# One half of the attention outputs divided on ScalarE instead of VectorE

## The chip, the core and the metric

The kernel runs on one core of a Trainium2 chip. The core has five engines with instruction streams of their own: TensorE (PE, matrix products, results into PSUM), VectorE (DVE), ScalarE (ACT), GpSimd (POOL) and SyncE (SP, which here only issues transfers). They wait for each other through semaphores. The metric is the device time of the whole program in microseconds (us), median of the runs shown.

## What is computed

Two sequences of 1024 tokens with 256 channels pass an attention layer, a residual with layer norm, a ternary linear layer and a second residual with layer norm:

```python
q = rmsnorm(rope(h @ Wq_c @ Wq_up), q_norm_w)       # 16 heads of 128
k_sw = rmsnorm(rope(h @ Wk), k_norm_w); v_sw = h @ Wv # one key/value head
ck = rmsnorm(h.reshape(b, nb, 16*256) @ W_comp)       # one key = value per 16 tokens
c_out  = attend(q @ ck^T * scale, blocks that end before the token, sink, ck)
sw_out = attend(50 * tanh(q @ k_sw^T * scale / 50), last 64 tokens, sink, v_sw)
attn = (c_out + sw_out in 4 groups @ Wg) @ Wo
x = layernorm(h + attn)
out = layernorm(x + x @ ternary(weight)^T + bias)
```

`attend` is a softmax with one more column, the head's sink, that takes part in the sum but has no value. Of importance here is `sw_out`, the window attention: the sum of exponentials times values, divided by the sum of the exponentials plus the sink's.

## The kernel before

**Tiles and stages.** After a preparation of some 75 us (keys, values, folded weights) the kernel goes through 16 tiles of 128 tokens. The function `step(i, front, mid, proj, ffn)` is written once for each engine and runs for i from -1 to 17. In one step, four tiles are under work: `front` makes the queries of tile i+1, `mid` does the attention of tile i, `proj` projects the attention output of tile i-1 and takes the first layer norm, `ffn` does the linear layer and second norm of tile i-2. The order on each engine is the order in which `step` issues its instructions; nothing reorders them. In this document "tile n" also names the step that has tile n in `mid`.

**Window attention of a tile.** The 128 tokens are two halves of 64 queries, c = 0 and 1. Each half sees 128 keys. With 16 heads a half has 1024 rows of scores; two heads of 64 queries fill 128 partitions, so a half is eight pairs. PE makes the scores (L582), ACT takes tanh and exp (L810, L814) into `E`, POOL multiplies by the mask (`mask(c)`, L1213) into `Pm`, and PE multiplies each pair by the values (`values(c)`, L665). A pair's result is 128 x 129 in PSUM: 128 output columns and, as the last one, the sum of the exponentials. The eight pairs lie in banks 4, 6 and 5, three, three and two in a bank, and both halves use the same three banks.

**Division (`divide(c)` on DVE).** DVE waits for the products (`p_pv`), adds the sink's term `e1` to the sums (`dn`, L1088), in half 0 also takes the reciprocals `rc` of the block attention's sums (L1092), takes the reciprocals `r8` (L1094), and multiplies the pairs by them with two instructions, 768 and 256 columns (`quotients`, L1102), into the float tile `ao`. `ao` and `Pm` lie in one room, which the trace names `room_wg`; `r8` is `r` in the trace and `room_wo` holds `PcT`, `y` and `x1`. `d_ao` tells that the half is done. Half 0 is rounded to 16 bits by ACT (`narrow` into `ao16[:, 0]`, L705, named `ao` in the trace, signals `a_at`); half 1 is rounded by DVE itself with a second pair of multiplications before the float one (`d_hi`).

**After it.** POOL takes the rounding rest of each half (`output_low(c)`, L1203). SP sends the 16-bit parts through transposing transfers to `aoT`, and PE projects them in the next step (L634 and L642). PE may write half 1's products over the banks only when half 0 has left them.

**Between the two divisions on DVE** stand `query_rest` (L1116, the low parts of the next tile's queries; SP then sends them through a transposing transfer, and the next tile's window scores need it), the residual `y` and the statistics of the first layer norm (L1130 to L1140). On ACT, `narrow` of half 0 stands between the rounding of the next queries (`query_high`, L705 into `room_K`) and the copy of the transposed block probabilities `PcT` (`a_ct`, L705 into `room_wo`), which waits for PE (L683). The order on POOL in a full step is: `mask(0)`, `mask(1)`, the block probabilities' division (L1227, longer with the tile's number in its sequence), `output_low(0)`, the power -1/2 for the layer norms (L1234, waits for `d_nl`), `x1` (L1238), `x1b` (L1242), `output_low(1)`, the result of the second norm (L1247), and, in the next step, the power for the queries' norm (L1219) and `mask(0)` again. PE transposes `x1` (L554) ahead of the next window scores, and ACT rounds that (L705 into `room_h`) ahead of the second of its two squares of the queries (L774), which DVE sums (L1017).

A tile attends to 1 to 8 groups of 8 blocks, by its place in its sequence, so the block parts (L616, L823, L1227) grow from tile 0 to 7 and again from 8 to 15.

## Time and profile before

| | us |
|---|---|
| median of 3 runs | 425.68 |
| lowest, highest | 423.60, 427.05 |
| the profiled execution | 423.94 |
| its span (first to last instruction) | 421.9 |

The profiled execution's span leaves 2.0 us around it. The mean granted TensorE clock was 0.965 of full speed. Tiles 0 to 15 run from about 77 to 402 us of the span, which is some 20 us a tile. In the rows below, "busy" excludes waiting, an idle time in brackets is that of the engine just before the row with what ended it, and rows of one line that follow each other are merged (x2: two instructions; the time is from the first start to the last end). The start of a merged row is that of its first instruction. A row without a bracket followed the one before it on its engine without a wait worth showing.

### The profile page before, as it was taken

The numbers are of one execution on the slowest core, as the hardware profiler recorded it, in microseconds if no ns is written. First come the engines' busy times: TensorE is split into PE (matmuls) and PEld (weight loads), VectorE is DVE, ScalarE is ACT, GpSimd is POOL, SyncE is SP. The second block draws the span as 40 slices with busy tenths as digits, with TensorE's granted clock in tenths as the row PEclk, the third lists the DMA queues.
The fourth block names the chain that finished last, engine by engine and source line by source line (L and its number), as shares of the span: only waits on it lengthen the run. The fifth ranks groups of instructions, "written<-read, shape, count | busy, mean of one in ns | idle before, by whom it ended". The sixth has DMA issues, their size and how long they took to land.

```text
span 421.9 us, 8693 instructions
## 1 busy us (share of the span) xinstructions
PE 367.2 (87%) x3111; PEld 298.4 (71%) x3111; DVE 345.4 (82%) x695; ACT 275.7 (65%) x802; POOL 302.5 (72%) x190
## 2 busy tenths in 40 slices
PE   6997798868978899989999999989798999989681
PEld 5995586566757777677878786858586777858570
DVE  2677799768898999999989898999999999963411
ACT  4558765857694959586958575776859595946200
POOL 1755280366796979888888877897979898986805
PEclk9899999959999999999999999999999999999995
DMA  7993005588775767879577777796857677675240
GB/s 247 319 255 109 1 0 86 215 260 126 114 102 101 112 118 97 139 100 125 95 128 92 118 98 120 108 126 123 129 101 114 112 102 132 89 135 71 41 73 25
DMA packets 148234, 50.19 MB, mean 119 GB/s; under 512 B 136544, under 2 KB 146784, under 8 KB 147936
## 3 DMA queue, kind: packets, MB, share of 16 engines
q1 hardware_dynamic: 147376, 49.31, 65.6%
q8 instruction: 25, 0.41, 0.4%
q10 hardware_dynamic: 816, 0.33, 0.3%
q14 instruction: 17, 0.14, 0.1%
HBM read 11.87 MB, written 4.19 MB: 38 GB/s over the span
## 4 chain that ended last, share of the span: by engine, by line
PE 33%; DVE 23%; issue 12%; DMA 10%; ACT 10%; POOL 9%; SPq 1%; POOLq 0%; ACTq 0%; DVEq 0%
PE PS L665 8%; ACT room_h L823 6%; PE PS L582 6%; DMA aoT<-ao 5%; PE PS L616 4%; DMA room_h<-room_K 4%; DVE ao L1102 4%; PE PS L634 3%; DVE room_K L1116 3%; DVE room_wg L1102 3%; PE PS L432 3%; PE PS L642 2%; PE PS L594 2%; DVE PS L1072 2%; POOL ao L1203 2%
## 5 line engine op out<-in xcount | busy, mean ns | idle before, releaser
L1203 POOL TENSOR_TENSOR ao<-room_wg,ao 128x1024 f16<-128x1024 f32 x32 | 68.2, 2132 | 25.1 <-ACT ao L705 18.1
L665 PE MATMUL PS<-V,room_wg 128*128 128x129 f32 x512 | 68.3, 287 | 9.4 <-POOL room_wg L1213 4.9
L1213 POOL TENSOR_TENSOR room_wg<-room_comp,keep 128x1024 f32<-128x1024 f32 x32 | 74.7, 2356 | 1.1 <-ACT room_comp L814 1.1
L665 PEld LDWEIGHTS PS<-V,room_wg 128*128 128x128 f32 x512 | 64.3, 200 | 14.4 <-POOL room_wg L1213 7.8
L823 ACT ACTIVATE room_h<-PS,room_K 128x8 f32<-128x8 f32 (+7 forms) x256 | 70.4, 362 | 1.8 <-DVE room_K L1043 1.7
L634 PE MATMUL PS<-Weff,aoT 128*128 128x256 f16 x512 | 58.5, 272 | 5.3 <-DMA aoT<-ao 5.1
L823 ACT ACTIVATION_READ_ACCUMULATOR room_h<-PS,room_K 128x1 f32 x256 | 62.0, 248 | 0.0
L1219 POOL TENSOR_TENSOR ny<-nx,nu 128x16 f32<-128x16 f32 x16 | 46.8, 2922 | 18.5 <-DVE nx L1019 18.4
L634 PEld LDWEIGHTS PS<-Weff,aoT 128*128 128x128 f16 x512 | 49.4, 98 | 13.3 <-issue 7.4
L582 PE MATMUL PS<-room_h,kT 128*128 128x512 f16 x192 | 44.2, 379 | 7.7 <-DVE room_wg L1102 6.2
L705 ACT ACTIVATE room_wo<-PS 128x128 f32<-128x128 f32 (+7 forms) x16 | 10.4, 651 | 49.1 <-PE PS L683 49.1
L1102 DVE TENSOR_TENSOR room_wg<-PS,r 128x768 f32<-128x768 f32 x64 | 41.1, 683 | 0.8 <-DVE r L1094 0.2
L810 ACT ACTIVATE room_comp<-PS 128x512 f32<-128x512 f32 x64 | 37.1, 600 | 5.2 <-PE PS L582 3.8
L472 PE MATMUL PS<-wqup_p,xcT 128*128 128x512 f32 x128 | 36.3, 420 | 3.1 <-POOL wqup_p L1174 2.5
L582 PEld LDWEIGHTS PS<-room_h,kT 128*128 128x128 f16 x192 | 17.5, 97 | 30.4 <-issue 7.7
L1017 DVE TENSOR_REDUCE ssq<-room_wg 128x8 f32<-128x1024 f32 x30 | 35.6, 1216 | 3.5 <-ACT room_wg L774 2.8
L1116 DVE TENSOR_TENSOR room_K<-PS,room_K 128x1024 f16<-128x1024 f32 x32 | 37.8, 1220 | 0.5
L1072 DVE TENSOR_TENSOR PS<-PS,ny 128x1024 f32<-128x1024 f32 x32 | 37.7, 1225 | 0.0
L705 ACT ACTIVATE room_K<-PS 128x1024 f16<-128x1024 f32 x32 | 33.2, 1059 | 2.9 <-DVE PS L1072 2.2
L616 PE MATMUL PS<-CW,room_wo 128*128 128x256 f32 (+1 forms) x144 | 34.9, 389 | 0.0
L774 ACT ACTIVATE room_wg<-PS 128x1024 f32<-128x1024 f32 x30 | 30.5, 1022 | 4.9 <-PE PS L472 4.6
L1227 POOL TENSOR_TENSOR room_h<-room_h,room_K 128x112 f32<-128x112 f32 (+7 forms) x16 | 22.0, 1372 | 15.2 <-DVE room_K L1092 15.2
(179 smaller groups left out, 754.9 us busy)
## 6 DMA issues: line engine op xcount, KB each, us to landing
H<-in_L_attn_h SPq DMA_DIRECT2D x4, 512.0 KB, 6.2
room_wg<-in_L_attn_Wg SPq DMA_DIRECT2D x1, 2048.0 KB, 13.2
cw_rows<-staged SPq DMA_DIRECT2D x1, 2048.0 KB, 6.4
CW<-cw_rows SPq DMA_DIRECT2D x1, 2048.0 KB, 8.0
out<-room_wo SPq DMA_DIRECT2D x16, 128.0 KB, 2.7
CW<-in_L_attn_Wq_up SPq DMA_DIRECT2D x2, 512.0 KB, 13.5
room_wo<-in_L_attn_Wo SPq DMA_DIRECT2D x1, 1024.0 KB, 15.1
room_h<-room_K SPq DMA_TRANSPOSE x64, 3.2
```

Of the source, the lines that this page charges most:

```text
L582: last = nc.tensor.matmul(bank(b), kT[:, kp, at + c * WIN:at + c * WIN + P], qT[:, qp, 8 * hf:8 * hf + 8, c * WIN:(c + 1) * WIN], start=n ...
L616: last = nc.tensor.matmul(o, PcT[0:rows, g, :], CW[0:rows, TPB * (t // TPB) + g, :], start=start and g == 0, stop=not start and g == end)
L634: last = nc.tensor.matmul(o, aoT[:, 0, hd % 2, hd // 2, :], Weff[:, wp, hd, :], start=mid and hd == wp == 0, stop=False)
L665: last = nc.tensor.matmul(pv, Pm[:, c, 2 * pr:2 * pr + 2, :], V[:, 2 * i + c, :], start=True, stop=True)
L705: nc.scalar.activation(dst, src, ACT.Copy).then_inc(s, 1)
L823: last = nc.scalar.activation(Ec[:, 0:n, hd], bank(4 + hd // 8)[:, (hd % 8) * n:(hd % 8 + 1) * n], ACT.Exp, bias=mn[:, hd:hd + 1], accum_o ...
L1072: V_.tensor_tensor(by_head(hf), by_head(hf), ny[:, heads].unsqueeze(2).to_broadcast([P, 8, D]), ALU.mult).then_inc(d_qn, 1)
L1102: last = V_.tensor_tensor(o, pv, r, ALU.mult)
L1116: V_.tensor_tensor(qp[:, 1, heads, :], by_head(hf), qp[:, 0, heads, :], ALU.subtract).then_inc(d_ql, 1)
L1203: G.tensor_tensor(ao16[:, 1, :, c, :], ao[:, c, :, :], ao16[:, 0, :, c, :], ALU.subtract).then_inc(g_al, 1)
L1213: G.tensor_tensor(Pm[:, c, :, :], E[:, c, :, :], keep[:, :, :], ALU.mult).then_inc(g_mask, 1)
L1219: G.tensor_tensor(ny[:, 0:HEADS], nx[:, 0:HEADS], nu[:, 0:HEADS], ALU.pow).then_inc(g_rs, 1)
```

## The change

Half 0 of each tile is divided on ACT. DVE's `divide(0)` ends after the reciprocals and signals `d_r8`. ACT waits for that and scales the eight pairs one by one, each with `nc.scalar.mul` of 128 x 128 out of PSUM, whose scale is a column of `r8` (one value per partition). Then it signals `a_dv`, waits for it itself, and rounds `ao[:, 0]` as before. PE's second half of products waits for `a_dv` in place of `d_ao`. DVE's `divide(1)` waits for `a_dv` before it overwrites `r8`; its wait for `g_al` now stands between its two pairs of multiplications, with the same count. `d_ao` counts one a tile, for half 1 alone, and all who wait for it are renumbered. The wait of POOL's rest for half 0 (`a_at`) is as before.

```diff
--- before.py
+++ after.py
@@ -195,12 +195,12 @@
 
 
 
-        a_sq, a_tanh, a_es, a_ec, a_qt, a_ct, a_at, a_xt = (sem(n) for n in (
-            "a_sq", "a_tanh", "a_es", "a_ec", "a_qt", "a_ct", "a_at", "a_xt"))
+        a_sq, a_tanh, a_es, a_ec, a_qt, a_ct, a_at, a_xt, a_dv = (sem(n) for n in (
+            "a_sq", "a_tanh", "a_es", "a_ec", "a_qt", "a_ct", "a_at", "a_xt", "a_dv"))
 
         d_nq, d_nl, g_rs = sem("d_nq"), sem("d_nl"), sem("g_rs")
-        d_red, d_qn, d_rope, d_add, d_cmax, d_rc, d_ql, d_ao, d_fr, d_y, d_hi, d_xl = (sem(n) for n in (
-            "d_red", "d_qn", "d_rope", "d_add", "d_cmax", "d_rc", "d_ql", "d_ao", "d_fr", "d_y", "d_hi", "d_xl"))
+        d_red, d_qn, d_rope, d_add, d_cmax, d_rc, d_ql, d_ao, d_fr, d_y, d_hi, d_xl, d_r8 = (sem(n) for n in (
+            "d_red", "d_qn", "d_rope", "d_add", "d_cmax", "d_rc", "d_ql", "d_ao", "d_fr", "d_y", "d_hi", "d_xl", "d_r8"))
 
         g_mask, g_cn, g_al, g_rl, g_x1, g_xb, g_out = (sem(n) for n in (
             "g_mask", "g_cn", "g_al", "g_rl", "g_x1", "g_xb", "g_out"))
@@ -549,7 +549,7 @@
                     pe.wait_ge(g_x1, i - 1)
                     wait(pe, d_fr, i - 2)
                     if not mid:
-                        pe.wait_ge(d_ao, 2 * NT)
+                        pe.wait_ge(d_ao, NT)
                     for k in range(KC):
                         last = nc.tensor.transpose(x1_bank(mid)[:, k * P:(k + 1) * P],
                                                    x1[:, k * P:(k + 1) * P], ident[:, :])
@@ -576,7 +576,7 @@
                     pe.wait_ge(s_qt, 64 * i + 64)
                     at = i * P + (i // TPB) * WIN
                     for u, b in enumerate((6, 4, 5, 6)):
-                        wait(pe, *((a_tanh, 4 * i + 1) if u == 3 else (d_ao, 2 * i)))
+                        wait(pe, *((a_tanh, 4 * i + 1) if u == 3 else (d_ao, i)))
                         c, hf = divmod(u, 2)
                         for n, (kp, qp) in enumerate(PARTS):
                             last = nc.tensor.matmul(bank(b), kT[:, kp, at + c * WIN:at + c * WIN + P],
@@ -657,7 +657,7 @@
                         if ffn:
                             pe.wait_ge(d_fr, i - 1)
                     else:
-                        pe.wait_ge(d_ao, 2 * i + 1)
+                        pe.wait_ge(a_dv, i + 1)
                     for pr in (3, 4, 5, 0, 1, 2, 6, 7):
                         if c == 0 and pr in (0, 6):
                             pe.wait_ge(a_ec, 2 * i + 1 + pr // 6)
@@ -830,7 +830,13 @@
                 if i == -1:
                     value_weights(act, lambda dst, src: nc.scalar.mul(dst, src, v_unit), 0)
                 if mid:
-                    act.wait_ge(d_ao, 2 * i + 1)
+                    act.wait_ge(d_r8, i + 1)
+                    wait(act, g_al, 2 * i - 1)
+                    for pr in range(PAIRS):
+                        pv = bank((4, 6, 5)[pr // 3])[:, (pr % 3) * VW:(pr % 3) * VW + D]
+                        last = nc.scalar.mul(ao[:, 0, pr, :], pv, r8[:, pr:pr + 1])
+                    last.then_inc(a_dv, 1)
+                    act.wait_ge(a_dv, i + 1)
                     wait(act, s_ah, 32 * i)
                     narrow(ao16[:, 0, :, 0, :], ao[:, 0, :, :], a_at)
                     act.wait_ge(p_ct, i + 1)
@@ -1091,8 +1097,11 @@
                         wait(dve, g_cn, i)
                         V_.reciprocal(rc[:, :], sc[:, :]).then_inc(d_rc, 1)
                     after_link()
+                    if c == 0:
+                        V_.reciprocal(r8[:, :], dn[:, :]).then_inc(d_r8, 1)
+                        return
+                    dve.wait_ge(a_dv, i + 1)
                     link(V_.reciprocal(r8[:, :], dn[:, :]))
-                    wait(dve, g_al, 2 * i + c - 1)
 
                     def quotients(dst):
 
@@ -1102,11 +1111,11 @@
                             last = V_.tensor_tensor(o, pv, r, ALU.mult)
                         return last
 
-                    if c:
-                        wait(dve, s_ah, 32 * i)
-                        quotients(ao16[:, 0, :, c, :]).then_inc(d_hi, 1)
-                    quotients(ao[:, c, :, :]).then_inc(d_ao, 1)
-                    dve.wait_ge(d_ao, 2 * i + c + 1)
+                    wait(dve, s_ah, 32 * i)
+                    quotients(ao16[:, 0, :, 1, :]).then_inc(d_hi, 1)
+                    wait(dve, g_al, 2 * i)
+                    quotients(ao[:, 1, :, :]).then_inc(d_ao, 1)
+                    dve.wait_ge(d_ao, i + 1)
 
                 def query_rest(hf):
 
@@ -1198,7 +1207,7 @@
                     if c == 0:
                         pool.wait_ge(a_at, i + 1)
                     else:
-                        pool.wait_ge(d_ao, 2 * i + 2)
+                        pool.wait_ge(d_ao, i + 1)
                     wait(pool, s_al, 32 * i)
                     G.tensor_tensor(ao16[:, 1, :, c, :], ao[:, c, :, :], ao16[:, 0, :, c, :], ALU.subtract).then_inc(g_al, 1)
 
```

On ACT, a full step of tile 1, from the exponentials of the block scores to the squares of the next queries. `room_K` is the rounded query, `room_wg` the tile `ao` (and the squares), `ao` the rounded output, `room_wo` the transposed probabilities. Before:

```order
L823 ACTIVATE room_h,room_K<-PS,room_K 128x16 x16
L705 ACTIVATE room_K<-PS 128x1024 x2
L705 ACTIVATE ao<-room_wg 128x8x128
L705 ACTIVATE room_wo<-PS 128x256
L774 ACTIVATE room_wg<-PS 128x1024
L705 ACTIVATE room_h<-PS 128x256
L774 ACTIVATE room_wg<-PS 128x1024
```

With the change:

```order
L823 ACTIVATE room_h,room_K<-PS,room_K 128x16 x16
L705 ACTIVATE room_K<-PS 128x1024 x2
L837 ACTIVATE room_wg<-PS,r 128x128 x8
L705 ACTIVATE ao<-room_wg 128x8x128
L705 ACTIVATE room_wo<-PS 128x256
L774 ACTIVATE room_wg<-PS 128x1024
L705 ACTIVATE room_h<-PS 128x256
L774 ACTIVATE room_wg<-PS 128x1024
```

Eight instructions stand ahead of the rounding of half 0; all that follow keep their order.

On DVE, the same place of a later tile: from the norm of the next queries over `divide(0)` and `query_rest` to the layer norm's statistics (`dn` and `r` are the sums and reciprocals of the division). Before:

```order
L1072 TENSOR_TENSOR PS<-PS,ny 128x1024 x2
L1088 TENSOR_TENSOR dn<-PS,e 128x6
L1088 TENSOR_TENSOR dn<-PS,e 128x2
L1092 RECIPROCAL room_K<-room_K 128x16
L1094 RECIPROCAL r<-dn 128x8
L1102 TENSOR_TENSOR room_wg<-PS,r 128x768
L1102 TENSOR_TENSOR room_wg<-PS,r 128x256
L1116 TENSOR_TENSOR room_K<-PS,room_K 128x1024 x2
L1130 SCALAR_TENSOR_TENSOR room_wo<-PS,o_inv,H 128x256
L1133 BN_STATS bns<-room_wo 128x6
```

With the change (its line numbers are those of the changed file):

```order
L1078 TENSOR_TENSOR PS<-PS,ny 128x1024 x2
L1094 TENSOR_TENSOR dn<-PS,e 128x6
L1094 TENSOR_TENSOR dn<-PS,e 128x2
L1098 RECIPROCAL room_K<-room_K 128x16
L1101 RECIPROCAL r<-dn 128x8
L1125 TENSOR_TENSOR room_K<-PS,room_K 128x1024 x2
L1139 SCALAR_TENSOR_TENSOR room_wo<-PS,o_inv,H 128x256
L1142 BN_STATS bns<-room_wo 128x6
```

The two multiplications between the reciprocals and the low parts of the queries are gone; nothing comes in their place.

## Rows read from the trace of the kernel before

**Rows 1.** The page, busy time of each engine: us, share of the span, instructions.

```profile
PE 367.2 (87%) x3111; PEld 298.4 (71%) x3111; DVE 345.4 (82%) x695; ACT 275.7 (65%) x802; POOL 302.5 (72%) x190
```

**Rows 2.** Who waited for whom, whole span: us in total, times, longest us.

```profile
ACT room_wo L705 <- PE PS L683: 49.1, 16, 4.5
...
ACT ao L705 <- DVE room_wg L1102: 19.0, 16, 2.6
```

**Rows 3.** The same view, POOL alone, from 88 to 400 us.

```profile
POOL ao L1203 <- ACT ao L705: 18.1, 16, 2.1
...
POOL ny L1234 <- DVE nx L1140: 10.6, 15, 1.6
```

**Rows 4.** Timeline of tile 12: start us, us, engine, line, op; idle before and its end.

```profile
327.20 2.15 ACT L705 ACTIVATE room_K<-PS 128x1024 f16<-128x1024 f32 x2
...
328.51 0.16 DVE L1094 RECIPROCAL r<-dn 128x8 f32<-128x8 f32 x1
...
328.71 1.29 DVE L1102 TENSOR_TENSOR room_wg<-PS,r 128x768 f32<-128x768 f32 x2
...
330.03 1.06 ACT L705 ACTIVATE ao<-room_wg 128x1024 f16<-128x1024 f32 x1 [0.67 <-DVE room_wg L1102]
330.03 2.35 DVE L1116 TENSOR_TENSOR room_K<-PS,room_K 128x1024 f16<-128x1024 f32 x2
331.16 2.13 POOL L1203 TENSOR_TENSOR ao<-room_wg,ao 128x1024 f16<-128x1024 f32 x1 [0.98 <-ACT ao L705]
...
331.48 1.95 PE L665 MATMUL PS<-V,room_wg 128*128 128x129 f32 x16
...
333.63 0.22 DVE L1088 TENSOR_TENSOR dn<-PS,e 128x6 f32<-128x6 f32 x2
...
333.81 0.70 POOL L1234 TENSOR_TENSOR ny<-nx,nu 128x2 f32<-128x2 f32 x1 [0.51 <-DVE nx L1140]
...
334.61 1.23 POOL L1238 TENSOR_SCALAR room_wo<-room_wo,mv,ny 128x256 f32<-128x256 f32 x1
...
336.64 1.02 ACT L774 ACTIVATE room_wg<-PS 128x1024 f32<-128x1024 f32 x1
336.65 2.35 DVE L1017 TENSOR_REDUCE ssq<-room_wg 128x8 f32<-128x1024 f32 x2
...
342.89 4.67 POOL L1213 TENSOR_TENSOR room_wg<-room_comp,keep 128x1024 f32<-128x1024 f32 x2
...
345.30 1.94 PE L665 MATMUL PS<-V,room_wg 128*128 128x129 f32 x14 [0.28 <-POOL room_wg L1213]
```

**Rows 5.** Timeline of ACT in the preparation, two evacuations that follow each other.

```profile
50.23 0.37 ACT L763 ACTIVATE ckTs<-PS,wqk 128x128 f16<-128x128 f32 x1 [1.54 <-DVE ckTv L959]
50.50 4.01 ACT L709 ACTIVATE room_wgT<-PS 128x512 f32<-128x512 f32 x8
```

**Rows 6.** Groups of ACT by shape: count, busy us, mean ns; idle before.

```profile
L705 ACT ACTIVATE room_wo<-PS 128x512 f32<-128x512 f32 x2 | 1.2, 599 | 4.7 <-PE PS L683 4.7
...
L705 ACT ACTIVATE room_wo<-PS 128x128 f32<-128x128 f32 x2 | 0.6, 277 | 7.0 <-PE PS L683 7.0
```

**Rows 7.** Timeline of tile 11, ACT and DVE.

```profile
307.16 2.15 ACT L705 ACTIVATE room_K<-PS 128x1024 f16<-128x1024 f32 x2
...
309.34 0.16 DVE L1094 RECIPROCAL r<-dn 128x8 f32<-128x8 f32 x1
```

**Rows 8.** Timeline of POOL, tile 7.

```profile
235.07 0.70 POOL L1234 TENSOR_TENSOR ny<-nx,nu 128x2 f32<-128x2 f32 x1 [1.19 <-DVE nx L1140]
```

**Rows 9.** Timeline of tile 5, DVE.

```profile
187.96 0.23 DVE L1088 TENSOR_TENSOR dn<-PS,e 128x6 f32<-128x6 f32 x2 [0.58 <-PE PS L665]
```

**Rows 10.** Chain of waits before tile 5: start us, us, what.

```profile
176.52 5.83 DMA aoT<-ao
...
182.48 3.65 PE PS L634 x32
```

**Rows 11.** Timeline of PE, tile 0, second half's products.

```profile
92.00 3.53 PE L665 MATMUL PS<-V,room_wg 128*128 128x129 f32 x16 [1.97 <-DVE room_wg L1102]
```

## The prediction

> **What bounds the kernel now.** I read the page first. PE is busy 87% of the span, VectorE (DVE) 82%, GpSimd (POOL) 72%, ScalarE (ACT) 65% [rows 1]. Read as shares this says: take from DVE, give to ACT. The waits say where ACT has room: it waits 49.1 us in 16 tiles for PE's transposed block probabilities, and, just ahead of that, 19.0 us for DVE's quotients [rows 2]. So ACT's own time is covered. Whether its result may come later is another question, and for that I follow who waits for the rounded half 0. It is POOL: 18.1 us in 16 tiles, and soon after POOL waits once more, for the layer norm's statistics, but only 10.6 us in 15 tiles [rows 3].
>
> The timeline of tile 12 shows the loop this makes [rows 4]. DVE takes the reciprocals at 328.51 and ends the quotients at 330.00. ACT rounds from 330.03 to 331.09, POOL makes the rest from 331.16 to 333.29, waits 0.51 us for the statistics, and starts the power for the norms at 333.81. From there it has no wait through x1 (334.61), the rest of half 1, the result and the power for the queries, up to the mask of the next tile at 342.89, whose first half (half of 4.67) ends at 345.2. PE waited 0.28 us for just that and starts the values at 345.30. That leads to the next reciprocals. So **POOL closes a loop around the tile with 0.51 us of play**, and the play lies right behind the instruction that the change delays. Of the fifteen tiles with this wait [rows 3], nine show 0.49 to 0.51 us; tile 7 has 1.19 [rows 8].
>
> **The price of the eight copies.** The trace has one ACT instruction of this form, 128 x 128 out of PSUM with a scale from a tile: 0.37 us long, and the next one started 0.27 us after it [rows 5]. Eight in a row take 7 x 0.27 + 0.37 = 2.26 us. Bounds: from above no overlap at all, 8 x 0.37 = 2.94. From below, instructions without a scale tile: eight of 512 columns take 4.01 us, which with a last one of 0.60 is 0.49 apart [rows 5, 6]; a column costs (599 - 277) / 384 = 0.84 ns [rows 6], so at 128 columns 0.49 - 0.32 = 0.17 apart and 7 x 0.17 + 0.28 = 1.5 us. I take 2.26, since its row has the same shape and operands. The two instructions that they replace took 1.29 us [rows 4].
>
> The Trainium skill ("ScalarE: Activation LUTs", section "What ACT_TABLE_LOAD costs") has for an ACTIVATE 186 ns plus 0.833 ns a column, 93 ns more for each pointer operand, and an overlap of 93 ns between neighbours. By that a copy is 0.386 us, 0.293 apart, eight are 2.44, and the sum below would be some 1.2 us larger (0.18 in seven tiles), 431.9. The row agrees with its form and lies a little under it (0.37 and 0.27).
>
> **When they end.** They start when the reciprocals are there (0.2 us after the start of L1094) and ACT has ended the queries' rounding, which stands ahead of them. In tile 11 ACT ends at 309.31, before the reciprocals of 309.34: ACT is free [rows 7]. In tile 12 it ends at 329.35, 0.84 after the start of the reciprocals at 328.51: ACT is late [rows 4]. With 0.05 us for ACT's wait for its own last write:
> - ACT free: the rounding starts 0.2 + 2.26 + 0.05 = 2.5 us after the start of L1094, not at 1.52 (330.03 - 328.51). **1.0 us later.**
> - ACT late: 0.84 + 2.26 + 0.05 = 3.15. **1.6 us later.**
>
> POOL's rest starts as much later. Its play takes 0.5 of it; the power, x1 and all behind it move by **0.5 us (free) or 1.1 us (late)**. Beside it, DVE's sum of the second squares needs x1 by way of PE and ACT. In tile 12, x1 is there at 335.84, ACT squares from 336.64 to 337.66, and DVE's second sum starts at about 337.8 (336.65 and half of 2.35) [rows 4]: play of some 0.1 us. So DVE moves too.
>
> **What it gives back.** DVE has 1.29 us less to do in each tile. Its work between the divisions runs without a wait in tile 12 from 328.5 to the sums at 333.63 [rows 4], so the statistics and the low parts of the queries come up to 1.3 us earlier, and the half-1 quotients by as much as PE's second products allow. PE starts these at 331.48; they now wait for ACT to 331.6 (late), so half 1 ends about where it did. With ACT free it ends 0.4 to 0.6 us earlier. But none of it starts POOL earlier, since POOL still has half 0's rest to do first. I cost this gain at nothing, except where a tile hangs on the transfer of the outputs. Tile 5 is such a one: 5.83 us of transfer, then 3.65 us of projection end ahead of its products, and DVE waited 0.58 us for them [rows 9, 10].
>
> **The sum, tile by tile,** with the same reading of each tile (ACT free or late, the play behind it, what else sets its end):
> - Tile 0: no projection stands between PE's halves, and PE waited 1.97 us for the quotients [rows 11]. They start with the last copy, 2.45 us after the start of the reciprocals, not with the quotients' end, 1.5 us after it (330.00 - 328.51 [rows 4]): +0.9.
> - Tiles 1 and 2: ended by the output transfer and by the low parts of the queries, which come no later: 0.
> - Tile 3, late by about 0.5: +0.65. Tiles 4 and 5: POOL's loss lies under the output transfer or the block exponentials but for +0.2 and +0.3.
> - Tiles 6 to 8, 14 and 15: seven or eight block groups, PE and ACT set the end, and POOL's play is larger (1.19 in tile 7 [rows 8]): 0.
> - Tile 9, free: +0.6. Tile 10: half 1's transfer starts earlier, -0.2. Tile 11: now late, since DVE reaches its reciprocals sooner than PE did: +0.95. Tile 12, late: +1.0. Tile 13: late, in part under the exponentials: +0.6.
> - After tile 15 the play is as in tile 7: 0.
>
> Sum: 0.9 + 0.65 + 0.2 + 0.3 + 0.6 - 0.2 + 0.95 + 1.0 + 0.6 = **+5.0 us**, on the profiled execution 423.94 + 5.0 = 428.9. That execution lies 1.7 us under the median of 425.68; the median is forecast at 425.7 + 5.0 = **430.7 us**.
>
> **Rivals.**
> 1. *The loss fits into the play.* If the copies follow each other at the lower bound (1.5 us), the rounding is late by 0.2 (free, wholly inside 0.51) or 0.85 (late, 0.35 beyond). Then tile 0 costs 0.1, tiles 3, 11, 12 and 13 together 1.2: 425.7 + 1.3 = 427.0. For it: the bare instruction is that cheap. Against: the row with a scale tile. Chance 0.22.
> 2. *Faster: DVE is the loop.* In eight tiles (2 to 4 and 9 to 13) DVE goes through from one division to the next without a wait, as in tile 12 [rows 4]. If that is what holds the tile and POOL merely follows it, each of the eight gets back some 1.1 us of the 1.29, as PE's second products allow: 8 x 1.1 = 8.8, 416.9 us. It decides at the point where the rounding comes less than 0.51 us later than now, that is, eight copies within 1.8 us with ACT free; beyond it POOL is the later one. For it: DVE's 82% and the unbroken rows. Against: PE's wait for POOL at 345.30, and POOL's unbroken rows ahead of it. Chance 0.10.
> 3. *Larger loss.* The copies don't overlap (2.94 us), each tile that pays does so with 0.7 more, and tiles 2, 4, 5 and 10 join: 5.0 + 7 x 0.7 = 9.9, 435.6 us. Chance 0.10.
>
> That ACT isn't where the change needs it can't be: the copies stand on its list in every tile, and their wait is for DVE alone.
>
> The forecast keeps 0.58, with a range of its own of 428.4 to 433.0. The range for 8 in 10 reaches down over rival 1 and up over half of rival 3: **424.0 to 434.0 us**; it leaves out rival 2 and the far end of rival 3. A change under 1% (4.3 us) can't be told from none with this kernel's scatter. The forecast lies just beyond that (1.2%), so about three fifths of its chance count as slower (0.36), with rival 3 0.46; the rest of it and most of rival 1 as the same (0.45), rival 2 as faster (0.09).
>
> **What would show it.** In the changed profile: the copies 0.37 us long and 0.27 apart; DVE's busy time down by 16 x 1.3 = 21 us; the rounding of half 0 2.5 to 3.2 us after the start of the reciprocals; POOL's wait for ACT's rounding up from 18.1 to about 36 us, and its wait for the statistics gone in all tiles but 6 to 8, 14 and 15; between tiles 11 and 14, reciprocals more than 20 us apart where it was 19.2 to 19.8. I am wrong if the copies are shorter, if POOL still waits for the statistics in tile 12, or if the next tile's reciprocals don't move when POOL's mask does.

## The result and the profile after

The changed kernel took **432.91 us** in the median (431.73 to 434.23), the kernel before 425.31 beside it on the same chip: 7.6 us more, ratio **1.020 [1.017, 1.023]**. Forecast were 430.7, or 5.0 us more. The time lies in the range and the sign is the forecast's; the loss is half as large again. Here and below, medians are over all executions, while the ratios leave out those in a slower state (more than 1.5% above the fastest of their kernel), so the two can differ by half a per cent. The profiled execution took 432.81 us with a span of 430.3; its page, the busy time of each engine:

```profile
PE 370.1 (86%) x3109; PEld 297.9 (69%) x3111; DVE 338.2 (79%) x663; ACT 309.4 (72%) x930; POOL 302.3 (70%) x190
```

Against [rows 1], ACT has 33.7 us more. DVE has only 7.2 less, where the forecast said 21: the first sign that something is wrong. The waits, who waited for whom over the whole span:

```profile
POOL ao L1212 <- ACT ao L705: 36.4, 16, 3.1
ACT room_wo L705 <- PE PS L683: 34.7, 16, 3.7
...
DVE room_wo L1139 <- PE PS L616: 16.4, 11, 4.3
```

and POOL's alone from 88 to 408 us, which answers to [rows 3]:

```profile
POOL ao L1212 <- ACT ao L705: 36.4, 16, 3.1
...
POOL ny L1243 <- DVE nx L1149: 0.9, 2, 0.6
```

POOL's wait for the rounded half 0 is up from 18.1 to 36.4 us, and its wait for the statistics is down from 10.6 to 0.9. DVE has a wait that was 1.9 us before and is now 16.4, for PE's projection of the previous tile's output (L616). The copies, group of ACT by shape (count, busy us, mean ns; idle before):

```profile
L837 ACT ACTIVATE room_wg<-PS,r 128x128 f32<-128x128 f32 x128 | 34.9, 399 | 2.0 <-DVE r L1101 1.9
```

The timeline of tile 12 answers to [rows 4] (start us, us, engine, line, op; idle before and its end):

```profile
332.83 0.16 DVE L1101 RECIPROCAL r<-dn 128x8 f32<-128x8 f32 x1
332.90 2.32 DVE L1125 TENSOR_TENSOR room_K<-PS,room_K 128x1024 f16<-128x1024 f32 x2
...
333.56 2.17 ACT L837 ACTIVATE room_wg<-PS,r 128x128 f32<-128x128 f32 x8
...
335.77 1.06 ACT L705 ACTIVATE ao<-room_wg 128x1024 f16<-128x1024 f32 x1
...
335.88 2.02 PE L665 MATMUL PS<-V,room_wg 128*128 128x129 f32 x16
336.00 0.48 DVE L1139 SCALAR_TENSOR_TENSOR room_wo<-PS,o_inv,H 128x256 f32<-128x256 f32 x1 [0.78 <-PE PS L616]
...
336.90 2.14 POOL L1212 TENSOR_TENSOR ao<-room_wg,ao 128x1024 f16<-128x1024 f32 x1 [2.40 <-ACT ao L705]
...
337.26 1.80 DVE L1149 TENSOR_SCALAR nx<-mv 128x2 f32<-128x2 f32 x1
...
338.98 0.22 DVE L1094 TENSOR_TENSOR dn<-PS,e 128x6 f32<-128x6 f32 x2
339.14 0.69 POOL L1243 TENSOR_TENSOR ny<-nx,nu 128x2 f32<-128x2 f32 x1
...
341.22 0.44 PE L554 MATMUL PS<-ident,room_wo 128*128 128x128 f32 x2 [0.72 <-POOL room_wo L1247]
...
342.10 2.75 PE L582 MATMUL PS<-room_h,kT 128*128 128x512 f16 x12 [0.44 <-DVE room_wg L1111]
...
350.63 2.18 PE L665 MATMUL PS<-V,room_wg 128*128 128x129 f32 x16 [0.22 <-POOL room_wg L1222]
```

In the kernel before, the row that matters below stood here, 0.27 us behind the end of POOL's rest at 333.29 [rows 4]:

```profile
333.56 0.17 DVE L1140 TENSOR_SCALAR nx<-mv 128x2 f32<-128x2 f32 x1
```

The eight copies take 2.17 us, the rounding starts 2.94 us after the reciprocals (before: 1.52) and POOL's rest of half 0 4.07 after them (before: 2.65). So far it is as forecast. What is new is the row of 337.26: DVE's last statistics instruction, an addition of a constant to two numbers in each partition, takes **1.80 us where it took 0.17**. It starts 0.36 us into POOL's rest and ends at 339.06, with POOL's rest at 339.04. Half 1's division stands behind it on DVE: its first row starts 6.15 us after the reciprocals, not 5.12, and the next tile's scores (PE L582) 9.27 after them, not 8.25, behind a wait for the quotients. The same instruction over all tiles:

```profile
L1149 DVE TENSOR_SCALAR nx<-mv 128x2 f32<-128x2 f32 x15 | 17.0, 1134 | 0.5
```

It was 0.17 in each of the 15. It is now long in eleven, by tile 2 to 7, 9 and 11 to 14: 2.13, 2.03, 1.81, 0.90, 0.90, 0.38, 2.13, 1.91, 1.80, 1.44, 0.90. The sum is 14.5 us more than fifteen rows of 0.17, which is what DVE's busy time lacks: 21 less 14.5 is 6.5, and 7.2 were read. A row that waits for its operands shows as idle time; this one waited after it had begun, and shows as work.

One stretch more differs, in the two single rows of tile 14's scores, after and before:

```profile
383.11 4.44 PE L582 MATMUL PS<-room_h,kT 128*128 128x512 f16 x12 [0.44 <-DVE room_wg L1111]
```

```profile
376.65 2.75 PE L582 MATMUL PS<-room_h,kT 128*128 128x512 f16 x12 [0.89 <-DVE room_wg L1102]
```

and the windows from reciprocal to reciprocal there (PE, PEld, DVE, ACT, POOL busy, granted clock, DMA share, GB/s):

```profile
373.90:396.60 22.70, 19.47 (x168) 15.05 (x168) 9.98 (x23) 14.34 (x50) 14.83 (x9) 0.92 0.60 100
```

```profile
367.70:388.50 20.80, 17.91 (x169) 14.74 (x168) 10.85 (x26) 12.28 (x42) 14.83 (x9) 1.00 0.72 109
```

The twelve products are the same, and in that window the granted clock is 0.92, not 1.00: most of these products ran at the lower of TensorE's two levels (1.2 against 2.4 GHz). The tile is 1.97 us longer. I come back to this.

The time from one tile's reciprocals to the next, against before, in us (rounded to 0.1; the row "without the block" is the experiment nx below):

| tile | 0 | 1 | 2 | 3 | 4 | 5 | 6 | 7 | 8 | 9 | 10 | 11 | 12 | 13 | 14 |
|---|---|---|---|---|---|---|---|---|---|---|---|---|---|---|---|
| forecast | 0.9 | 0 | 0 | 0.65 | 0.2 | 0.3 | 0 | 0 | 0 | 0.6 | -0.2 | 0.95 | 1.0 | 0.6 | 0 |
| after | 1.0 | -0.2 | 0 | 0.8 | 0.6 | 0.2 | 0.3 | 0 | 0 | 0.5 | -0.3 | 0.7 | 1.0 | 0.8 | 2.0 |
| without the block | 1.0 | 0.3 | -0.3 | 0.4 | -0.5 | 0 | 0 | 0 | 0 | 0.2 | -0.4 | 0.5 | 0.4 | 0.2 | 0 |

Before rounding, the three rows sum to +5.0, +7.5 and +1.8 us.

### The profile page after: what moved, and what is told of

It is laid out like the page before. It is cut to its first block, busy times and chain, and to the rows that moved or that the text cites. A ratio compares the mean times of both kernels' runs of the same rounds, so it can differ in the third digit from the quotient of the medians.

```text
span 430.3 us, 8803 instructions
## 1 busy us (share of the span) xinstructions
PE 370.1 (86%) x3109; PEld 297.9 (69%) x3111; DVE 338.2 (79%) x663; ACT 309.4 (72%) x930; POOL 302.3 (70%) x190
## 4 chain that ended last, share of the span: by engine, by line
PE 32%; DVE 21%; POOL 15%; issue 14%; ACT 13%; DMA 4%; SPq 1%; POOLq 0%; ACTq 0%; DVEq 0%
PE PS L665 7%; ACT room_h L823 6%; PE PS L582 6%; PE PS L616 5%; POOL ao L1212 4%; DVE ao L1111 4%; PE PS L642 4%; POOL room_wg L1222 3%; DVE room_wg L1111 3%; DMA aoT<-ao 3%; ACT room_wg L837 3%; PE PS L432 2%; PE PS L594 2%; PE PS L634 2%; POOL ny L1228 2%
## 5 line engine op out<-in xcount | busy, mean ns | idle before, releaser
L1212 POOL TENSOR_TENSOR ao<-room_wg,ao 128x1024 f16<-128x1024 f32 x32 | 68.3, 2133 | 41.9 <-ACT ao L705 36.4
L582 PE MATMUL PS<-room_h,kT 128*128 128x512 f16 x192 | 46.0, 389 | 6.2 <-DVE room_wg L1111 6.2
L582 PEld LDWEIGHTS PS<-room_h,kT 128*128 128x128 f16 x192 | 17.9, 99 | 29.9 <-issue 10.9
L837 ACT ACTIVATE room_wg<-PS,r 128x128 f32<-128x128 f32 x128 | 34.9, 399 | 2.0 <-DVE r L1101 1.9
L616 PE MATMUL PS<-CW,room_wo 128*128 128x256 f32 (+1 forms) x144 | 35.2, 391 | 0.0
L814 ACT ACTIVATE room_comp<-room_comp 128x1024 f32<-128x1024 f32 x32 | 31.9, 1048 | 0.0
```

Of the source, the lines that this page charges most:

```text
L582: last = nc.tensor.matmul(bank(b), kT[:, kp, at + c * WIN:at + c * WIN + P], qT[:, qp, 8 * hf:8 * hf + 8, c * WIN:(c + 1) * WIN], start=n ...
L616: last = nc.tensor.matmul(o, PcT[0:rows, g, :], CW[0:rows, TPB * (t // TPB) + g, :], start=start and g == 0, stop=not start and g == end)
L837: last = nc.scalar.mul(ao[:, 0, pr, :], pv, r8[:, pr:pr + 1])
L1212: G.tensor_tensor(ao16[:, 1, :, c, :], ao[:, c, :, :], ao16[:, 0, :, c, :], ALU.subtract).then_inc(g_al, 1)
```

## The experiments

Two theories stood at the start, and I held the first. **Late rest**: the loss is POOL's, as forecast, and the long DVE row is a side effect that costs little. **Block**: DVE's freed time brings its statistics instruction under POOL's rest, where it can't go on, and that is the larger part. Each ratio is against the kernel before, run on the same chip, with its 95% interval.

**1. d8: the copies on top of the kernel before.** Half 0 stays divided on VectorE; eight ACT copies of the same size are put ahead of the rounding, which overwrites what they write.

```diff
                 if mid:
-                    act.wait_ge(d_ao, 2 * i + 1)
+                    act.wait_ge(d_rc, i + 1)
                     wait(act, s_ah, 32 * i)
+                    wait(act, g_al, 2 * i - 1)
+                    for pr in range(8):
+                        last = nc.scalar.mul(ao16[:, 0, pr, 0, :], ident[:, :], qw[:, 0:1])
+                    last.then_inc(a_dv, 1)
+                    act.wait_ge(a_dv, i + 1)
+                    act.wait_ge(d_ao, 2 * i + 1)
```

> The kernel before, with eight extra ScalarE copies (128 x 128, scale from a tile) between the start of the reciprocals and the rounding of half 0; VectorE still divides both halves, and PE's second products still wait for VectorE alone. The copies' results are overwritten. POOL-loop theory (the loss is that the rounding of half 0 reaches GpSimd 1.0 to 1.6 us late): about +5 to +6.5 us, nearly the whole of the change's +7.6. Rival, PE's second products wait for ScalarE's copies: this wait isn't here, so 0 to +1 us. GpSimd's wait for the layer norm's statistics should shrink as in the changed kernel, and the one-column-pair instruction for the statistics on VectorE (0.17 us before) should take 1 us and more, until GpSimd's rest of half 0 ends, if the two exclude each other.

Measured: 439.45, 1.032 [1.026, 1.038], 14.7 us more: far over what was expected. Its tile 12:

```profile
340.44 2.43 ACT L837 ACTIVATE ao<-ident,qw 128x128 f16<-128x128 f32 x8
...
342.91 1.06 ACT L705 ACTIVATE ao<-room_wg 128x1024 f16<-128x1024 f32 x1
...
344.04 2.14 POOL L1209 TENSOR_TENSOR ao<-room_wg,ao 128x1024 f16<-128x1024 f32 x1 [2.66 <-ACT ao L705]
...
344.75 1.46 DVE L1146 TENSOR_SCALAR nx<-mv 128x2 f32<-128x2 f32 x1
```

Without any relief of DVE, POOL's rest alone has moved over the statistics row, which is 1.46 us long here. So the block isn't tied to DVE being early; either side's move brings the two together, and this run measures both costs at once. There is a third cost in it. Its granted clock is 0.947 over the span, against 0.965, and the trace says where: tiles 1, 2, 9, 10 and 14 have 0.92 or 0.93, where the kernel before has 1.00. Tiles 0 to 14 are together 11.9 us longer than in d8nx (experiment 6, the same without the block, and with the lower clock in tile 1 alone), and tiles 2, 9, 10 and 14 hold 6.7 of it. So the 14.7 is no measure of the block alone.

**2. d4: four copies** instead of eight (`range(4)`).

> As the run with eight extra copies, but with four. They end 1.3 us (ScalarE free) to 2.1 us (ScalarE late) after the start of the reciprocals, where the quotients end at 1.5: the rounding comes 0 to 0.55 us late, and GpSimd has 0.51 us of play. POOL-loop theory: a threshold, so 0 to +1.5 us, much under half of the run with eight. If ScalarE's busy time itself were the cost, half of what eight cost, some +3 us.

Measured: 423.76, 1.000 [0.995, 1.004]. Its tile 12:

```profile
332.07 0.16 DVE L1100 RECIPROCAL r<-dn 128x8 f32<-128x8 f32 x1
...
332.81 1.27 ACT L837 ACTIVATE ao<-ident,qw 128x128 f16<-128x128 f32 x4
...
334.11 1.06 ACT L705 ACTIVATE ao<-room_wg 128x1024 f16<-128x1024 f32 x1
```

The rounding starts 2.04 after the reciprocals, 0.52 later than before, which is POOL's play, and later by less or as much in the other tiles. A delay of that size costs nothing. The profiled execution also shows what a stretch at the lower clock costs. It took 429.5 us, and it has a granted clock of 0.92 in tiles 10 and 14; these two are 1.98 and 1.69 us longer than before, and no other tile is more than 0.12 longer. In tile 10 it falls on the projection, which took 3.65 before:

```profile
305.43 5.32 PE L634 MATMUL PS<-Weff,aoT 128*128 128x256 f16 x32 [1.53 <-DMA aoT<-ao]
```

**3. nx: the changed kernel without the block.** The statistics are added up by another form of instruction: the constant stands as a third number beside mean and variance, and a reduction over the pair (variance, constant) gives the same sum.

```diff
+            V_.memset(mv[:, :, 2], 1e-5)
...
-                    V_.tensor_scalar(nx[:, HEADS + sets.start:HEADS + sets.stop], mv[:, sets, 1], 1e-5, None,
+                    V_.tensor_reduce(nx[:, HEADS + sets.start:HEADS + sets.stop], mv[:, sets, 1:3], AX.X,
                                      ALU.add).then_inc(d_nl, 1)
```

> The changed kernel, with the instruction that makes variance + epsilon for the layer norms written as a sum over the pair (variance, epsilon) and not as an addition of a constant. In the changed kernel's trace the addition takes 1.80 us in tile 12 (0.17 before) and ends with GpSimd's rest of half 0. If the form of the instruction is what lets GpSimd block it, the sum takes about 0.2 us, half 1 is divided up to 1.0 us earlier, and the window scores up to 0.4 us earlier. POOL-loop theory: GpSimd still has to end the rest of half 0 before it takes the roots, so only 0 to -2 us of the +7.6. Rival, the block on VectorE is the cause of the loss: -5 us or more.

Measured: 427.95, **1.007 [1.004, 1.011]**: 3.2 us over before, where the changed kernel has 7.6. Its page and its tile 12:

```profile
PE 368.5 (86%) x3111; PEld 298.7 (70%) x3111; DVE 324.6 (76%) x664; ACT 306.6 (72%) x930; POOL 301.4 (71%) x190
```

```profile
331.31 0.16 DVE L1102 RECIPROCAL r<-dn 128x8 f32<-128x8 f32 x1
...
334.04 1.06 ACT L705 ACTIVATE ao<-room_wg 128x1024 f16<-128x1024 f32 x1
...
335.18 2.13 POOL L1213 TENSOR_TENSOR ao<-room_wg,ao 128x1024 f16<-128x1024 f32 x1 [2.20 <-ACT ao L705]
...
335.75 0.16 DVE L1150 TENSOR_REDUCE nx<-mv 128x2 f32<-128x4 f32 x1
...
336.27 0.23 DVE L1095 TENSOR_TENSOR dn<-PS,e 128x6 f32<-128x6 f32 x2 [0.36 <-PE PS L665]
...
337.27 0.70 POOL L1244 TENSOR_TENSOR ny<-nx,nu 128x2 f32<-128x2 f32 x1
...
348.66 2.05 PE L665 MATMUL PS<-V,room_wg 128*128 128x129 f32 x16 [0.71 <-POOL room_wg L1223]
```

The reduction again starts under POOL's rest (0.57 us into it, the addition 0.36) and takes 0.16. DVE's busy time is down 20.8 us from before, as forecast. Half 1's division starts 4.96 after the reciprocals, the next scores 8.32 after them (changed kernel: 6.15 and 9.27), and PE waits 0.71 us for POOL's mask (L1223), where it waited 0.28 before [rows 4] and 0.22 in the changed kernel. POOL ends the wait in all three, as the prediction had it, but only here by a clear margin: in the changed kernel PE's own row comes nearly as late.

The form gives back 4.4 us by the medians and 5.3 by the ratios (the two intervals together leave 3 to 7). That is outside the 0 to -2 of the late-rest theory and about the 5 of its rival.

**4. order: POOL makes the rest of half 0 later,** behind x1.

```diff
-                    output_low(0)
                 if proj or ffn:
...
                 if mid:
+                    output_low(0)
                     output_low(1)
```

> The changed kernel, with GpSimd's rest of half 0 moved behind the first layer norm (x1 and x1 + bias), so that nothing of the norm waits for ScalarE's copies; both rests then follow each other. GpSimd's instructions up to the next mask stay the same in number. POOL-loop theory, in its form that GpSimd's unbroken row up to the next mask sets the tile: x1 comes 2 us earlier, but the mask starts about when it did (0.3 later to 0.2 earlier), so within 2 us of the changed kernel. Rival, the late x1 (through PE, ScalarE's squares and VectorE) is the cause: back to the time of the kernel before or under it, -6 to -9 us against the changed kernel.

Measured: 441.44, 1.035 [1.027, 1.043]. The two rows in which it pays, around tile 12:

```profile
346.03 0.69 POOL L1242 TENSOR_TENSOR ny<-nx,nu 128x2 f32<-128x2 f32 x1 [3.03 <-DVE nx L1149]
...
359.54 2.05 PE L665 MATMUL PS<-V,room_wg 128*128 128x129 f32 x16 [1.86 <-POOL room_wg L1222]
```

POOL now stands idle for 3.03 us until the statistics come, its work of 2.1 us moves whole behind x1, and PE waits 1.86 us for the mask. It takes the block away (the row is 0.17 again) but lengthens POOL's loop: tiles 7, 12 and 13 are 1.2 to 1.4 us longer than before. The lower clock is in it too, in tiles 8, 9, 11 and 14, so the 16.7 us over before aren't POOL's alone. Neither theory expected this, and it doesn't tell them apart; it shows that the early rest fills a hole on POOL that is needed.

**5. b_nx: the reduction in the kernel before** (the edit of 3 on before), to see whether the form matters by itself.

> The kernel before with the statistics' instruction as a sum over a pair. In the kernel before this instruction never falls into GpSimd's rest of half 0 (0.17 us each), so all theories say no change: -1 to +1 us. If the form itself gained time, part of what the same edit gave the changed kernel would not be due to the block.

Measured: 424.78, 0.998 [0.994, 1.002]. Nothing, as there nothing is blocked.

**6. d8nx: the edits of 1 and 3 together,** the late rest alone, without relief and without block.

> The kernel before with eight extra ScalarE copies ahead of the rounding of half 0 (results overwritten), and the statistics' instruction as a sum. It leaves of the change only the late rounding, with neither the block on VectorE nor VectorE's relief nor PE's wait for ScalarE. With eight copies and the old form it was +14.7. Theory of two causes (GpSimd's late rest, and the block of VectorE behind it): +4 to +6 us. Rival, the late rounding alone explains the +14.7, by way of TensorE's lower granted clock or of ScalarE's busy time: +10 us or more.

Measured: 430.39, 1.012 [1.005, 1.020], 5.3 us more (the interval leaves 2 to 8), against 14.7 in d8, with the block and the lower clock. Its tile 12:

```profile
336.80 2.15 POOL L1210 TENSOR_TENSOR ao<-room_wg,ao 128x1024 f16<-128x1024 f32 x1 [2.47 <-ACT ao L705]
...
337.71 0.16 DVE L1147 TENSOR_REDUCE nx<-mv 128x2 f32<-128x4 f32 x1
...
338.90 0.70 POOL L1241 TENSOR_TENSOR ny<-nx,nu 128x2 f32<-128x2 f32 x1
```

This is the prediction's late rest by itself. It forecast 4.1 for it (5.0 less the 0.9 of tile 0, a wait that isn't here), so the size fits, within a wide interval. The play shows tile by tile: in tile 9 the rounding comes 1.11 us later than before and the tile is 0.50 longer, in tile 11 it is 1.32 and 0.70. In these two some 0.6 us are free and the rest is paid. Its eight copies take 2.44 us, not 2.17.

**7 and 8. split and splitnx: a division that ends in time.** Both engines start at the reciprocals: DVE divides six pairs in two instructions, ACT the last two pairs; splitnx has the reduction as well.

```diff
+                        dve.wait_ge(d_r8, i + 1)
+                        wait(dve, g_al, 2 * i - 1)
+                        for k in range(2):
+                            last = V_.tensor_tensor(ao[:, 0, 3 * k:3 * k + 3, :], full[:, k, :, 0:D],
+                                                    r8[:, 3 * k:3 * k + 3].unsqueeze(2).to_broadcast([P, 3, D]), ALU.mult)
+                        last.then_inc(d_q0, 1)
                         return
...
-                    for pr in range(PAIRS):
+                    for pr in range(6, PAIRS):
```

> The changed kernel with six of the pairs of half 0 divided on VectorE (two instructions of 384 columns) and only two copied on ScalarE. The copies end 0.85 us (ScalarE free) or 1.5 us (late) after the start of the reciprocals, the six pairs after 1.0: the rounding is no later than in the kernel before, and up to 0.4 us earlier. If the loss is the late rounding with its two consequences, it is gone, and VectorE's 0.4 us a tile come through in six to eight tiles: -3 to 0 us against the kernel before. Rival, any work on ScalarE between the reciprocals and the rounding costs: +1 to +3 us.

> As the split kernel, with the statistics' instruction as a sum. In the split kernel that instruction comes 0.4 us earlier and may meet the last 0.2 to 0.3 us of GpSimd's rest in the tiles where ScalarE is late; the sum isn't blocked. -3.5 to 0 us against the kernel before, 0 to 1 us under the split kernel.

Measured: split 419.72, **0.982 [0.974, 0.990]**; splitnx 422.35, 0.992 [0.988, 0.996]. Tile 12 of split:

```profile
324.06 0.16 DVE L1103 RECIPROCAL r<-dn 128x8 f32<-128x8 f32 x1
...
324.25 1.02 DVE L1107 TENSOR_TENSOR room_wg<-PS,r 128x384 f32<-128x384 f32 x2
324.79 0.62 ACT L838 ACTIVATE room_wg<-PS,r 128x128 f32<-128x128 f32 x2
...
325.44 1.06 ACT L706 ACTIVATE ao<-room_wg 128x1024 f16<-128x1024 f32 x1
326.58 2.14 POOL L1220 TENSOR_TENSOR ao<-room_wg,ao 128x1024 f16<-128x1024 f32 x1 [0.85 <-ACT ao L706]
...
328.71 0.17 DVE L1157 TENSOR_SCALAR nx<-mv 128x2 f32<-128x2 f32 x1
...
328.96 0.70 POOL L1251 TENSOR_TENSOR ny<-nx,nu 128x2 f32<-128x2 f32 x1 [0.24 <-DVE nx L1157]
```

The rounding starts 1.38 after the reciprocals, 0.14 earlier than before, and POOL waits again for the statistics (0.24). They start with POOL's rest at its end and are not blocked (0.17), so the reduction has nothing to remove. Both times miss what was expected: split gained more than 3 us, and splitnx came 2.6 us above it, not under it. The traces show no such difference. Tiles 1 to 13 are together 3.3 us shorter than before in either; splitnx has the lower clock in tile 14, for 1.7 us.

**9. nx0: nx with tile 0 divided on VectorE,** since tile 0's loss is of another kind (PE waits for the copies).

> The changed kernel with the sum form (no block), and tile 0 alone divided on VectorE again, in three instructions (1.4 us). In the changed kernel PE's second products of tile 0 start 2.52 us after the start of the reciprocals, in the kernel before 1.63. Theory: tile 0's term of the sum, -0.7 to -0.9 us against the run with the sum form alone (+3.2 us), thus +2.3 to +2.5 against the kernel before, and the step from tile 0 to 1 back from 19.8 to 19.0. Rival, TensorE is cold there and tile 0 hides the wait: no difference, +3.2.

Measured: 426.0, 1.007 [1.003, 1.010] against nx's 1.007. In the trace tile 0's step is back from 19.82 to 18.86 us (18.81 before); the time doesn't resolve it.

**10 to 12. split3 (three pairs on ACT), split_r (split again), again (the changed kernel again),** on a third chip.

> The split kernel with three pairs on ScalarE and five on VectorE (384 and 256 columns). The three copies take 0.88 us: with ScalarE free the rounding starts 1.1 to 1.2 us after the reciprocals, with ScalarE late 1.7, which is 0.2 later than in the kernel before and inside GpSimd's play, but the statistics, now 0.6 earlier, meet the end of GpSimd's rest in those tiles (a block of 0.3 to 0.5 us). Theory: -1 to +1 us against the split kernel, -4 to -7 against the kernel before. Rival, what counts is VectorE's time alone: 0.2 us less in each of 16 tiles, -3 us against the split kernel.

> The split kernel again, with more rounds, on another chip job: a ratio of 0.980 to 0.992 against the kernel before, as the run with a ratio of 0.982 and the same kernel with the sum form (0.992) gave.

> The changed kernel again, +7 to +8 us against the kernel before. In the first trace the window scores of tile 14 took 4.44 us at a lower granted clock, where the kernel before took 2.75. If the change causes this, it stands in this trace too; if it comes and goes between executions, tile 14 takes 2.75 here and the block's signature (the statistics' instruction of 0.9 to 2.1 us in tiles 2 to 6, 9 and 11 to 14) stands alone.

Measured: split3 421.22, 0.992 [0.988, 0.997]; split_r 422.08, 0.997 [0.994, 1.000], above the 0.980 to 0.992 that was expected; again 433.4, 1.024 [1.017, 1.031]. The loss of the change repeats, with the same tiles blocked. Against split_r beside it, split3 is 0.9 us faster, as the theory had it (-1 to +1); against before it gained 3.9, just short of what was expected. The gain of the split has the same sign both times, but it is 1.8% in the first run and 0.3% in the second, where it isn't clear of none. By the times alone: between no gain and 2%. The traces are steadier. Tiles 1 to 13 are 3.3 us shorter than before in split and 3.6 in split_r, of which 0.7 is chance in the trace of before (b_nx has that too): 2.6 to 3 us are left, or 0.6 to 0.7%.

## Why the prediction was half right

**The place and the play held.** 0.52 us later costs nothing (d4), 1.1 to 1.6 us later costs 5.3 (d8nx), and by d8nx's tiles the limit is at some 0.6, near the 0.51 that I read. Rival 1, the loss inside the play, falls with this, and so does rival 2: POOL's wait for the statistics vanished, and no tile gained more than 0.3. Rival 3 needed copies that don't overlap, and they do; the loss went its way for another reason.

**The price of the copies held,** 2.17 us for 2.26. They are 0.25 us apart, not 0.27, and 0.36 to 0.42 long. (The upper bound, 8 x 0.37, is 2.96 and not 2.94; nothing hangs on it.) The Trainium skill's rule ("ScalarE: Activation LUTs", "What ACT_TABLE_LOAD costs") would have given 2.44 for them, as an estimate; the trace disagrees for copies out of PSUM. For the copies of d8, from one SBUF tile to another and with 16-bit results, 2.43 was measured, which agrees.

**When they end held:** the rounding comes 2.4 (ACT free) to 2.95 us (late) after the reciprocals, for 2.5 and 3.15. POOL's wait for it came to 36.4 us, for 36. Tile 0 lost 1.0 for 0.9.

**What failed is the step "What it gives back",** where I cost the earlier statistics at nothing. The step saw that they come up to 1.3 us earlier (they come 0.62 earlier in tile 12; PE's projection, 0.78 us of wait, holds the rest) and asked only whether that starts POOL earlier. It didn't ask what runs on POOL at the place they come to. Before, POOL's rest and the row were 0.27 us apart. The change moves POOL's rest later by 1.4 and the row earlier by 0.6, and they overlap. The step's other reading, that half 1 ends about where it did, fails with it: its division starts 6.15 after the reciprocals, not 5.12. The Trainium skill names a mechanism that fits ("SBUF — State Buffer", "Who interferes with whom"): DVE's copies and tensor_scalar forms can use a second pair of ports that it shares with GpSimd, and whoever issues first holds it for its whole instruction, while a tensor_reduce never contends. The traces agree at this place: 1.80 us for the one form, ending with POOL's row, and 0.16 for the other. What no run here shows is that it is the ports. And at another place the block doesn't last for POOL's whole instruction. DVE's multiply-add on 128 x 16 numbers (0.17 us where POOL is idle) meets POOL's result row, here in tile 12 of the changed kernel:

```profile
344.15 1.22 POOL L1256 TENSOR_SCALAR room_wo<-room_wo,mv,ny 128x256 f32<-128x256 f32 x1
344.37 0.35 DVE L1025 TENSOR_SCALAR nx<-ssq 128x16 f32<-128x16 f32 x1
```

It ended 0.57 us after POOL's start, with 0.65 of POOL's row to go. Begun 0.59 us into that row it took 0.17 (nx, tile 6), and begun 0.87 into it 0.39, to POOL's end (the changed kernel, tile 7).

**The sum in parts,** by timed medians: the late rest alone +5.3 (d8nx); from there to nx -2.1, which is DVE's relief and copies 0.27 us shorter, less tile 0's wait for the copies (+1.0, not in d8nx); the block +4.4 (the changed kernel against nx; by the ratios +5.3). That these make 7.6 is no proof, as each is the step from one run to the next. The first and the last are clear of the noise; the -2.1 isn't, for the intervals of d8nx and nx overlap. The traces have the same signs: tiles 1 to 14 sum to +4.5 in d8nx (0.9 of it in tile 1, which has the lower clock) and to +0.8 in nx, and from nx to the changed kernel tiles 0 to 14 grow by 5.7, 2.0 of it in tile 14.

The forecast's late rest has about the right size. It lacked the other two parts, of which the relief wasn't nothing either: in nx ACT is late by 0.64 us and not 0.84 in tile 12, and tiles 4 and 10 gain 0.4 to 0.5. The block undoes this: half 1's division comes later, with it the next tile's scores and so ACT's rounding of the queries, and ACT is 0.84 late again, which is where the copies start. That the tiles of the changed kernel match the forecast's one by one (table) is therefore partly luck: the block filled the place of a loss that the rest and the relief together wouldn't have made. Where the tile sums miss, it is tiles 4, 6 and 13, and above all 14.

**Open: tile 14.** Its products of the scores at the lower clock stand in the profiled executions of the changed kernel (both times), d8, d4, order and splitnx, and not in those of before, b_nx, nx, nx0, d8nx, split, split_r and split3. In the changed kernel, PE's idle 1.81 us for x1 and 0.44 for the quotients stand ahead of it, against 1.08 and 0.89 before. These waits alone don't bring it: d4 and splitnx have the drop with the same 1.08 or 1.07 and 0.89 or 0.90 ahead as the kernel before, splitnx without any block and d4 without one in this tile. Nor is it tied to tile 14: d8 has it in 1, 2, 9 and 10 too, d8nx in 1, order in 8, 9 and 11, d4 in 10, and the changed kernel's second trace in 1. d4's profiled execution took 429.5 us, while its timed median is 423.76. So it comes with some executions, and it is 1.7 to 2 us of the profiled one. How much of the block's 4.4 us it makes isn't settled. One such stretch lowers the mean clock of a span by some 0.004 (an estimate: 0.08 of 22.7 us in 430), and the means over the executions in the ratios, 0.961 for the changed kernel and 0.962 for nx, differ by less; that speaks for a small part. What brings the drop stays open.

## What to carry to other kernels

When an instruction's result comes later, look for the play right behind it, and when an engine is relieved, look at what its work slides under: both ends of an overlap can move. A VectorE row that is many times its usual length and ends with a GpSimd row is most likely blocked, not busy; another form of the same operation may be free of it. And if a second engine has room, give it the part that both finish by the old time (here two pairs of eight) rather than the whole.

## What the runs showed of the hardware

- An addition of a constant on DVE, 128 x 2 numbers from one SBUF tile to another, took up to 2.13 us beside a POOL operation of 2.13 us, and 0.17 without; the reduction of 128 x 4 numbers to the same result took 0.16 beside it. Beside this operation the small one always ended with it. Beside POOL's operation on 128 x 256 numbers (1.22 us), a multiply-add of 128 x 16 took 0.35, 0.17 or 0.39, by where in it it began.
- ACT copies of 128 x 128 with a scale tile follow each other after 0.25 us out of PSUM into 32-bit (2.17 for eight) and after 0.29 from SBUF into 16-bit (2.43 for eight).
- The granted clock of one tile was 0.92 in some executions and 1.00 in others, of the same kernel or nearly the same; the twelve products of the scores that take 2.75 us took 4.44, and the thirty-two of the projection 5.32 and not 3.65. In the run where nothing else differed (d4), such a tile was 1.7 to 2.0 us longer.
